# Value minus error, computed by GpSimd from ScalarE's copy of the error instead of by VectorE from PSUM

## What is computed

```python
rk = normalised heads of layernorm(x);  wk = rk shifted by one token
v = x @ Wv.T;  gate = sigmoid(x @ Wg.T);  beta = sigmoid(x @ Wb.T)
def step(S, t):                      # a state S of 32x32 per head and sequence
    pred = wk_t @ S
    err  = (v_t - pred) * b_t
    S    = S + outer(wk_t, err)
    o    = (rk_t @ S) * g_t
x = x + layernorm(attention(layernorm(x)))
x = x + layernorm(ffn(layernorm(x)))     # quantised activations times ternary weights
```

## Time and profile before

| what | value |
|---|---|
| median of 3 runs | 2561.44 us |
| the runs | 2545.59 to 2561.95 us |
| the profiled execution's time | 2552.82 us |
| its span, first to last instruction | 2551.1 us |
| its mean granted clock of TensorE, as a share of 2.4 GHz | 0.947 |
| busy share of the span, VectorE / TensorE / GpSimd / ScalarE | 88% / 85% / 68% / 67% |

### The profile page before, as it was taken

The page is one execution under the profiler, slowest core; times in us unless marked ns, Lnnn a source line. Parts: engine busy times, 40 slices in busy tenths (PEclk is TensorE's granted clock), DMA queues, the critical chain, the costliest instruction groups (busy, mean ns, idle before and its releaser), DMA issues. The chain is left out here.

```text
span 2551.1 us, 146840 instructions
## 1 busy us (share of the span) xinstructions
PE 2161.4 (85%) x61989; PEld 1350.0 (53%) x61989; DVE 2239.5 (88%) x6603; ACT 1699.0 (67%) x3372; POOL 1731.3 (68%) x2841
## 2 busy tenths in 40 slices
PE   1679999999999999999999989999998747777776
PEld 1356555556555565555655555556655524434442
DVE  4599999999999999999999999999999837777875
ACT  2667777777777777777777777777774335555554
POOL 1556777767777776777777767776775335777777
PEclk7789999999999999999999999999999868888888
DMA  2112222222222222222222222222222124565554
GB/s 79 51 46 63 71 79 76 75 71 72 78 72 78 72 75 72 75 78 71 75 76 78 72 71 78 77 74 71 73 66 62 53 95 146 152 162 153 153 139 99
DMA packets 132137, 215.50 MB, mean 84 GB/s; under 512 B 31352, under 2 KB 31360, under 8 KB 131488
## 3 DMA queue, kind: packets, MB, share of 16 engines
q1 hardware_dynamic: 131488, 206.20, 28.4%
HBM read 104.40 MB, written 67.11 MB: 67 GB/s over the span
## 5 line engine op out<-in xcount | busy, mean ns | idle before, releaser
L740 DVE TENSOR_TENSOR ps_elim<-ps_elim,sys 128x30 f32<-128x30 f32 (+14 forms) x1920 | 543.4, 326 | 0.8
L748 DVE TENSOR_TENSOR sys<-sys,ps_elim 128x30 f32<-128x30 f32 (+14 forms) x1920 | 534.4, 316 | 1.0
L893 PE MATMUL ps_v<-wv,xt 128*128 128x512 f16 x1536 | 433.5, 391 | 34.7 <-DMA kbd<-kt 20.5
L893 PE MATMUL ps_y<-wo,ot 128*128 128x512 f16 x1536 | 404.3, 387 | 12.4 <-DVE x L811 10.1
L1293 PE MATMUL ps_f<-wq,f_xq 128*128 128x512 f16 x1024 | 281.6, 426 | 102.1 <-ACT f_yn L1169 97.5
L920 PEld LDWEIGHTS ps_chain<-rhs,t_t 32*32 32x32 f32 x16384 | 263.1, 144 | 127.0 <-issue 121.7
L543 POOL TENSOR_TENSOR o_g<-pred,gate 128x512 f32<-128x512 f32 x128 | 134.3, 1049 | 286.1 <-DVE pred L827 286.1
L920 PE MATMUL ps_chain<-rhs,t_t 32*32 32x32 f32 x16384 | 294.5, 218 | 20.2 <-issue 12.8
L620 ACT ACTIVATE z<-x,z_sc 128x512 f32<-128x512 f32 x128 | 104.1, 814 | 265.4 <-POOL z_sc L519 265.4
L528 POOL TENSOR_TENSOR m_t<-gram,b_mask 128x512 f32<-128x512 f32 x128 | 164.3, 1283 | 147.7 <-ACT gram L627 141.7
L914 PEld LDWEIGHTS ps_chain<-state,key_t 32*32 32x32 f32 x16384 | 174.5, 105 | 158.2 <-issue 156.4
(11 more groups left out here) (155 smaller groups left out, 5157.7 us busy)
## 6 DMA issues: line engine op xcount, KB each, us to landing
x_in<-in_L_attn_x SPq DMA_DIRECT2D x128, 256.0 KB
kbd<-kt SPq DMA_DIRECT2D x512, 64.0 KB
x_res<-in_L_attn_x SPq DMA_DIRECT2D x128, 256.0 KB
x_scratch<-x SPq DMA_DIRECT2D x128, 256.0 KB, 6.4
f_x<-x_scratch SPq DMA_DIRECT2D x32, 1024.0 KB, 7.6
out<-f_res SPq DMA_DIRECT2D x128, 256.0 KB, 3.9
gate<-gates SPq DMA_DIRECT2D x128, 7.9 KB
gate<-gates SPq DMA_DIRECT2D x128, 0.2 KB
```

The costliest lines, as they stand in the source:

```text
L740: dve.tensor_tensor(tmp, factors(r, c, first, end)[:, c - first:C - 1 - first, c - first:c - first + 1].to_broadcast(shape), sys[:, r, c:c ...
L748: dve.tensor_tensor(dst, dst, tmp, ALU.add).then_inc(elim_done[r], 1)
L893: last = pe.matmul(out, lhs[:, a, kb, :], weights[:, w, kb, :], start=(i == 0), stop=(i == 3 * KB - 1))
```

## The change

VectorE's `pred` goes. GpSimd computes it from `val` and ScalarE's copy `err`, both in SBUF, right in front of `o_g`. `err` gets two buffers, and ScalarE's copy waits for `pred` of two chunks before. TensorE, which waited for `pred` before it wrote `ps_chain` again, waits for the error copy instead.

```diff
-        err = sb("err", [P, D])
+        err = sb("err", [P, 2, D])
...
                 n, l, live = on(base, j, 0)
                 if live:
+                    wait(pool, s["err_done"], n + 1)
+                    wait(pool, s["v_done"], n + 1)
+                    wait(pool, s["o_done"], n)
+                    pool.tensor_tensor(pred[:, :], val[:, l, :], err[:, l % 2, :], ALU.subtract).then_inc(s["pred_done"], 1)
                     wait(pool, s["pred_done"], n + 1)
...
                     wait(act, s["err_psum"], n + 1)
-                    wait(act, s["s_psum"], n)
-                    nc.scalar.activation(err[:, :], ps_chain[:, :], ACT.Copy).then_inc(s["err_done"], 1)
+                    wait(act, s["s_psum"], n - 1)
+                    wait(act, s["pred_done"], n - 1)
+                    nc.scalar.activation(err[:, l % 2, :], ps_chain[:, :], ACT.Copy).then_inc(s["err_done"], 1)
...
-                n, l, live = on(base, j, 0)
-                if live:
-                    wait(dve, s["err_done"], n + 1)
-                    wait(dve, s["o_done"], n)
-                    dve.tensor_tensor(pred[:, :], val[:, l, :], ps_chain[:, :], ALU.subtract).then_inc(s["pred_done"], 1)
-
...
-                    wait(pe, s["pred_done"], n)
+                    wait(pe, s["err_done"], n)
...
-                            last = pe.matmul(ps_s[q, e], key_b[q, l, e], err[q, e],
+                            last = pe.matmul(ps_s[q, e], key_b[q, l, e], err[q, l % 2, e],
```

## The result

| | before | after |
|---|---|---|
| median, us | 2561.69 (4 runs) | 2595.12 (4 runs, 2589.76 to 2597.81) |
| profiled execution: time, span | 2552.82, 2551.1 | 2589.76, 2588.0 |

The ratio is 1.0141, 95% interval 1.0095 to 1.0186: by it the change costs 36 us (24 to 48), and the two medians differ by 33. The forecast was 2594 us, +33.

The account below looks back on a forecast made before the run. A loop through VectorE, GpSimd and TensorE, beside VectorE's own, was taken to bound the kernel. 0.65 us a step x 0.44 x 115 steps gave +33 us on 2561.4: 2594 us, range 2535 to 2622.

Parts of the forecast that it names:

- the weight 0.44: Estimated crossings a step of the time-setting path through VectorE's changed stretch: one microsecond there costs 0.44 us a step.
- The engines take turns: VectorE operations on two SBUF tensors and GpSimd operations exclude each other, one operation each, around `z_ends` and the subtraction.
- The early step: First `z_ends` waits for GpSimd's `o_part`, the subtraction goes before the second: VectorE loses 0.48 us.
- The late step: First `z_ends` waits for the subtraction, the second for `o_g`: VectorE loses 1.30 us, taken as 1.20.
- The length of a VectorE step, +0.65 us: Forecast growth of VectorE's attention-loop step: 0.62 x 0.48 + 0.38 x 1.20 - 0.10 us.
- the share of 0.38 late steps: Share of steps with a late first `z_ends`, inferred from its 199 ns mean excess; 0.62 were taken as early.
- `g_den` gave 0.11 back: VectorE's `g_den`, held by GpSimd's `key`, was to become shorter with VectorE later: -0.10 us a step.
- The sum: 0.65 us a VectorE step times 0.44 gives 0.29 us a step, over 115 steps +33 us.
- GpSimd in the bound: Rival: VectorE's delay makes every first `z_ends` late and crossings rise to 0.6: +76 us, 2637; chance 0.10.
- The naive gain: Rival: no turns, the subtraction fits GpSimd's idle 2.0 us and VectorE saves 0.60 us: -30 us, 2531; chance 0.13.
- VectorE keeping its turn: Rival: VectorE holds its turn over both `z_ends`: -10 us, 2551; chance 0.27 together with VectorE's loss falling into TensorE-late steps.
- absorbed: Rival: VectorE's loss falls into TensorE-late steps, weight 0.2 or less: +15 us or less; chance 0.27 together with turn kept.

Follow-up runs that it names:

- e5: Kernel before plus one unneeded VectorE reduction of a constant tile behind its subtraction, 0.60 us of the engine, no GpSimd work: ratio 1.0136 to before, +35 us.
- e10: Kernel before with running maximum and minimum kept by one reduction over three tiles a step instead of the two `z_ends`; VectorE keeps the subtraction: ratio 1.0106, +27 us.
- e2: Kernel before with only the addition: GpSimd also subtracts, into a tile nobody reads, while VectorE keeps its subtraction: ratio 1.0353 to before, +90 us.
- e4: Changed kernel with the two `z_ends` replaced by one-tile reductions, running maximum and minimum not kept: ratio 0.9912 to the kernel before, -23 us.
- e3: Kernel before with the two `z_ends` replaced by one-tile reductions, running maximum and minimum not kept: ratio 0.9943 to before, -15 us.
- e9: Changed kernel with maximum and minimum kept by one reduction over three tiles a step, `err` back to one buffer: ratio 0.9974 to the kernel before, -7 us.
- e1: Changed kernel without GpSimd's subtraction: nobody subtracts and `o_g` reads the value itself: ratio 1.0003 to the kernel before.
- e11: The changed kernel repeated unaltered on another chip: ratio 1.0122 to the kernel before, +31 us.
- e7: Changed kernel with `z_ends` and residual moved behind the key norm's small operations in odd steps, in front of them in even steps: ratio 1.0217 to before.
- e8: Kernel before with `z_ends` and residual moved around the key norm's small operations, VectorE keeping the subtraction: ratio 1.0159 to before.

## Why the prediction was right

The sign, the mechanism and the time held, the last with help from terms that were off in opposite directions.

- **What bounds the kernel, and the weight 0.44.** Right, and rather low. Per microsecond of length, e5 measured 0.55 (0.42 to 0.68) and e10 0.52. The weight is no constant: e2's 1.20 us of length had 0.65, and e4's 0.61 us less, 70 us in 115 steps, brought 23 to 28 us, 0.3 to 0.4, with VectorE waiting for TensorE in 55 of 80 steps.
- **The engines take turns.** Right in each part. The early step was forecast to end L821 1.12 + 0.55 = 1.67 us after L819, and the trace has 1205.05 - 1203.37 = 1.68. The late step was forecast with ends at 0.55, 1.45 and 2.00 us after the subtraction's for L819, `o_g` and L821; the trace has 0.55, 1.47 and 2.01. e3 and e4, and e10 and e9, show that the loss goes when the turns at this place go; e1 and e2 show that neither the removal nor the addition behaves as it would without turns; and e10 shows that VectorE's longer step, without any more work on GpSimd, is enough for 27 of the 31 to 36 us.
- **The length of a VectorE step, +0.65 us, was too much**: it was +0.42. The stretch from `z_ends` to the key transpose grew by 0.58 us (2.58 against 2.00), not 0.75. What was off is the share of 0.38 late steps. It was 11 of 77, 0.14. In the trace of before 23 of 79 L819 started behind `o_part`, 0.29: in 7 more L819 was not held either, because it started in the last 0.17 us of `o_part`, and such a step loses as little as an early one. (16 L824 of after took over 1.3 us, but 5 of these are early ones that met nearly all of `o_part`.) In 11 other steps L824 ran in front of `o_part`, where the stretch is 0.37 us over the unheld 1.80. Why VectorE came late less often than before is not shown. `g_den` gave 0.11 back (281 to 170 ns), as forecast. The key norm's first small operation gave another 0.11 (386 to 280 ns) and another behind it took 0.05 (181 to 235). Both read two SBUF tensors and vary in length (161 to 1193 ns for the first, before), so the same turns are the likely reason; these two were left out of the sum.
- **The sum.** The length's change was put too high and the weight too low, and the two errors partly cancelled: that the forecast of +33 lies on the difference of the medians is in part luck. With the measured length and e5's weight it is 0.42 x 0.55 x 115 = 27 us, and e10's 27 us for 0.45 us say the same, against a measured 31 to 36 with intervals down to 24. The intervals do not require more. If something is missing, it may be on GpSimd's side: `b_mask` waited for `gates` in 66 of 78 steps, in the others GpSimd was itself late, and the mean from `gates` to the Gram copy in odd steps rose from 6.70 to 6.92 us (6.94 in e11, 6.70 in e10). So GpSimd in the bound, a rival with 0.10, is not the main cause, but some 4 to 9 us of it stay open, and e7 against e8 shows that it can cost more in another order.
- **The naive gain** fell with e1 and e2, and came true as soon as the turns at this place were gone: -30 us were its price, and e9 against e10 gave -34. e4 against e3 gave only -8 to -12. **VectorE keeping its turn** fell with L826's median of 1751 ns; the loss was not *absorbed* either, by e5 and e10.

## What to carry to other kernels

Before work is moved to an engine that has idle time, look at what the other engine does in that idle time: the time may be what lets a neighbour run. The sign to look for in the profile of before is a line whose duration varies, or differs from that of its twin next door (878 and 679 ns here), and what its partner runs at that moment. If two engines exclude each other, changing the operation of one may do more than changing its place: the same move that costs 1.2 to 1.4% beside the two-input `z_ends` gains 0.3% (e3 to e4) or 1.3% (e10 to e9) beside reductions. One SBUF input is not enough by itself. The TENSOR_SCALARs `f_z` and `g_den` read one SBUF tensor each and were held all the same. What these runs show unheld are reductions, the key transpose, and an operation with one operand in PSUM.

## What the runs showed of the hardware

- VectorE and GpSimd take turns even against a VectorE operation that is ready back to back: in the 78 steps of after, L826's duration is 1.53 to 1.76 us in all but one. In e11 it was short (0.68 us) in 7 of 77. In these 8 steps GpSimd had only its small operations of one column beside it (L452, L454), and VectorE had two turns in a row.
- A reduction of one SBUF tile was not held at all (672 to 675 ns on average beside running GpSimd operations, e3 and e4), and neither was the reduction over 1536 elements (1.90 to 1.92 us in all 128 steps of e9).
- Nor was a two-input operation with one operand in PSUM: `rhs` took 0.63 to 0.69 us in all 79 steps of before, with a large GpSimd operation beside it for over 0.3 us in 77 of them.
- A reduction that reads 1536 elements a row with a stride of 512 and writes 512 took 1907 ns, where the one of 512 contiguous elements took 675. No run has a contiguous one of 1536, so what the stride costs is not shown.
